# Forming the low halves of the expert weights on GpSimd instead of VectorE, and its high halves one step earlier

## The chip, the core and the metric

The kernel runs on one core of a Trainium2 chip. A core has five engines that run their own instruction streams and wait for each other on semaphores: TensorE (PE in the profile, with its weight loads as PEld), VectorE (DVE), ScalarE (ACT), GpSimd (POOL) and SyncE (SP, which only starts transfers here). The metric is device time in microseconds of one execution, the median of several. Smaller is better. TensorE writes to PSUM, the other memory is SBUF; in the profile a PSUM tensor of this kernel is called `bank`, everything else that a compute engine touches lies in SBUF.

## What is computed

A small language-model tower on 2 sequences of 2048 tokens: an embedding, a state-space mixer (Mamba-2 type) with a gated MLP, and a mixture of 8 experts with a shared one, at width 192. The change touches only how the weights of the last part are prepared.

```python
def _L0_ffn_ref(x, gate_weight, gate_bias, w1, w2, w3, sw1, sw2, sw3):
    ...
    h1 = jnp.einsum('td,eid->tei', x2, w1)
    h3 = jnp.einsum('td,eid->tei', x2, w3)
    h = jax.nn.silu(h1) * h3
    y = jnp.einsum('tei,edi,te->td', h, w2, cw)
    z = jax.nn.silu(x2 @ sw1.T) * (x2 @ sw3.T) @ sw2.T
    return (y + z).reshape(B, S, D)
```

Products with `w1`, `w3`, `sw1`, `sw3` and the router's weights are made on TensorE in float16. To keep float32 accuracy every weight matrix is held as two float16 parts: a high part (`w_hi`, the rounded weight) and a low part (`w_lo`, weight minus high part). A width of 192 is more than 128 partitions, so there is a second tensor for the rest of it: `wt_raw`, `wt_hi`, `wt_lo`. The columns COL_E to COLS, 2312 of them, belong to the shared expert, the eight experts and the router.

## The kernel before

**Staging.** The 2048 tokens are cut into 16 chunks of 128 (for both sequences at once). Each engine's program is `ramp()`, then `body(2, 1, 0)`, then a hardware loop over `body(i + 2, i + 1, i)` for i = 1 to 13, then `finale(14, 15)`. In `body(p, f, b)` three chunks are in work: chunk `b` is finished (MLP and experts), chunk `f` is in its scan, chunk `p` is begun (embedding, norm, input projection). The order of the instructions on each engine is written out by hand; nothing reorders them. A wait stops everything behind it on its engine.

**Preparing weights.** It happens once. The input projection's parts are made first in the ramp. The MLP's (`middle_weights`, 1536 columns) get their high part on ScalarE and their low part on VectorE (L1049), late in the ramp. The experts' high parts are made on GpSimd by `last_weights(hi, raw)` (L587 to L590): a copy of 2312 columns with conversion to float16, once for `w_hi` and once for `wt_hi`, as the last two instructions of GpSimd's ramp, behind `gate(0, 1)` and `halo(1)`. The experts' low parts are made on VectorE by its own `last_weights(wt, half)` (L1051 to L1057), four subtractions of 1156 columns each, which VectorE's `swiglu` (L1229 to L1250) places behind the gated products 0, 2, 3 and 5 of chunk 0 only (`not later(c)` is true in the first body alone). TensorE's `router` waits for all of them (`w_last_hi` 2, `w_last_lo` 4) before the first expert product of chunk 0.

**The work around it.** On VectorE: `convolve_tap` (xa, L1132) are the convolution taps of the new chunk, `masks` (mr, L1193) multiply the decay matrices `er` with the causal mask `gm` for the scan (units 0 to 5, 6 and 7 within `swiglu`, 8 to 11 behind it), `swiglu` forms `gt` from ScalarE's `sg` and a bank, `v_low` forms the low part of the MLP's input (v_t, L1071), `pre_low` that of the next chunk's input (u_t, the same line). On GpSimd: `decayed` (state, L503) and `gate` (y, L510) serve the scan, `weighted_x` (xw, L492) its state, `mixed` (rm, L516), `pre` and `norm2` (L445 and L447) are the powers of the three norms, `embed` (L458, L464) looks up the embedding rows by an indirect transfer. ScalarE's `mixed_norm` waits for rm; VectorE's `v_low` waits for it in turn; TensorE's `turn_v` and then `swiglu` wait for that. TensorE's first instruction of the scan of chunk 1 is the transposes of `scan_operands(1)` (L1647), which wait for ScalarE's `convolved_rest(1)` (xs, L716), which waits for the last tap (`xa_ready`).

Of the kernel before, what the change touches and what calls it, by code (L numbers as in the profile page):

```python
# [21 lines left out]
ALU = mybir.AluOpType  # L22
# [31 lines left out]
COL_E = COL_U + DM  # L54
# [25 lines left out]
def later(c):  # L80

    return not (isinstance(c, int) and c == 0)
# [20 lines left out]
def program(nc, tokens, position, table, weights, norms, conv_w, conv_b, shared_rows, d_skip, w_out, w_down,  # L103
            w2, identity, lower_ones, triangle_rows, exponent_rows, pair_rows, spread_rows, out):
    with ExitStack() as ctx:
# [332 lines left out]
        def _(pool):  # L438
# [67 lines left out]
            def gate(c, b):  # L506
                pool.wait_ge(y_sum[b], c + 1)
                pool.wait_ge(zs_ready[0], c + 1)
                pool.wait_ge(zs_ready[1], c + 1)
                pool.tensor_tensor(y[:, b], y[:, b], zs[:, :, b, :], ALU.mult).then_inc(y_ready[b], 1)  # L510
# [76 lines left out]
            def last_weights(hi, raw):  # L587
                x = slice(COL_E, COLS)
                pool.wait_ge(in_experts, 32)
                pool.tensor_copy(hi[:, x], raw[:, x]).then_inc(w_last_hi, 1)  # L590

            def ramp():
                pool.memset(xr[:, :, :, 0:KC - 1], 0.0).then_inc(setup_p, 1)
                embed(0)
                embed(1, 1)
                pre(0)
                keep(0)
                pool.memset(state[:], 0.0).then_inc(setup_p, 1)
                pool.memset(ones16[:], 1.0).then_inc(setup_p, 1)
                pool.memset(xd[:], 0.0).then_inc(setup_p, 1)  # L600
                pool.memset(bc[0:NS], 0.0).then_inc(setup_p, 1)
                pool.memset(bt[:, :, 0:NS], 0.0).then_inc(setup_p, 1)
                pool.wait_ge(setup_p, SETUP_P)
                pre(1)
                steps_decay(0)
                halo(0)
                embed(2)
                weighted_x(0, 0)
                weighted_x(0, 1)
                decayed(0, 0)  # L610
                steps_decay(1)
                gate(0, 0)
                decayed(0, 1)
                gate(0, 1)
                halo(1)
                last_weights(w_hi, w_raw)
                last_weights(wt_hi, wt_raw)

            def body(p, f, b):
                if f is not None:  # L620
                    weighted_x(f, 0)
                    weighted_x(f, 1)
                mixed(b)
                if f is not None:
                    pool.wait_ge(vl_turned, b + 1)
                    decayed(f, 0)
                    keep(f)
                    gate(f, 0)
                if p is not None:
                    pre(p)  # L630
                    embed(p + 1)
                norm2(b)
                if f is not None:
                    pool.wait_ge(xnt_done, b + 1)
                    decayed(f, 1)
                    gate(f, 1)
                if p is not None:
                    steps_decay(p)
                experts(b, p)
# [376 lines left out]
        def _(ve):  # L1016
# [31 lines left out]
                m = slice(COL_G, COL_E)  # L1048
                ve.scalar_tensor_tensor(lo[:, m], raw[:, m], scale, hi[:, m], ALU.mult, ALU.subtract).then_inc(w_rest_lo, 1)  # L1049

            def last_weights(wt, half):  # L1051

                ve.wait_ge(w_last_hi, 1 + wt)
                hi, lo, raw = (wt_hi, wt_lo, wt_raw) if wt else (w_hi, w_lo, w_raw)
                n = (COLS - COL_E) // 2
                x = slice(COL_E + half * n, COL_E + (half + 1) * n)
                ve.tensor_tensor(lo[:, x], raw[:, x], hi[:, x], ALU.subtract).then_inc(w_last_lo, 1)  # L1057

            def split(c, head, tail, src, hi, lo, lo_ready, lo_tail):


# [168 lines left out]
            def swiglu(c, p, f):  # L1230
                for t in range(NF):
# [13 lines left out]
                    if p is not None:  # L1245
                        if t == 1:
                            pre_add(p)
                            pre_stats(p)
                    if not later(c) and t in (0, 2, 3, 5):
                        last_weights(*divmod((0, 2, 3, 5).index(t), 2))  # L1250

            def second_input(c, src=p_out[0]):
                back_steps.start()
# [944 lines left out]
```

## Time and profile before

| | |
|---|---|
| three runs, median (lowest, highest) | 796.38 us (795.68 to 796.73) |
| the profiled execution, its own time | 796.69 us |
| its span in the profile | 794.9 us |
| busy in the span: PE, DVE, ACT, POOL | 757.6, 636.5, 546.8, 328.3 us |
| PE's share of the chain of work that ended last | 87% |

The span is what the engines' records cover; 1.8 us of the profiled execution's time lie outside it. Times in rows are microseconds from the span's start. In a timeline row the first number is the start, the second the duration (of the whole group if several instructions are merged, `x2`), and a bracket tells how long the engine had stood idle before and who released it. Ramp and first body take roughly the first 111 us; each further body takes some 46.6 us.

### The profile page before, as it was taken

The numbers are of one execution on the slowest core, as the hardware profiler recorded it, in microseconds if no ns is written. First come the engines' busy times: TensorE is split into PE (matmuls) and PEld (weight loads), VectorE is DVE, ScalarE is ACT, GpSimd is POOL, SyncE is SP. The second block draws the span as 40 slices with busy tenths as digits, with TensorE's granted clock in tenths as the row PEclk, the third lists the DMA queues.
The fourth block names the chain that finished last, engine by engine and source line by source line (L and its number), as shares of the span: only waits on it lengthen the run. The fifth ranks groups of instructions, "written<-read, shape, count | busy, mean of one in ns | idle before, by whom it ended". The sixth has DMA issues, their size and how long they took to land.

```text
span 794.9 us, 23059 instructions
## 1 busy us (share of the span) xinstructions
PE 757.6 (95%) x7278; PEld 646.6 (81%) x7278; DVE 636.5 (80%) x1691; ACT 546.8 (69%) x1242; POOL 328.3 (41%) x478
## 2 busy tenths in 40 slices
PE   2679999999999999999999999999999999999897
PEld 1556788988888898888888888888988888888786
DVE  4699987879788787978878797887889788786745
ACT  4975777767777776777767677776767777675533
POOL 5355544433444443344344334434443443442222
PEclk9899999999999999999999999999999999999999
DMA  7420000000000000000000000000000000000000
GB/s 251 155 89 1 12 22 12 9 25 6 15 10 21 10 6 25 3 17 10 21 10 6 25 3 17 10 21 10 6 24 4 17 10 16 14 6 11 2 1 21
DMA packets 14923, 18.93 MB, mean 24 GB/s; under 512 B 4656, under 2 KB 13008, under 8 KB 14448
## 3 DMA queue, kind: packets, MB, share of 16 engines
q1 hardware_dynamic: 13264, 15.25, 6.0%
q0 software_dynamic: 1632, 3.34, 1.7%
q8 instruction: 15, 0.25, 0.1%
q14 instruction: 12, 0.10, 0.0%
HBM read 14.39 MB, written 4.19 MB: 23 GB/s over the span
## 4 chain that ended last, share of the span: by engine, by line
PE 87%; DVE 2%; issue 1%; ACT 1%; POOL 0%; DVEq 0%; POOLq 0%; ACTq 0%
PE bank L1554 40%; PE bank L1934 11%; PE bank L1862 8%; PE bank L1718 6%; PE bank L1707 5%; PE bank L1831 4%; PE bank L1818 3%; PE bank L1809 3%; PE bank L1795 2%; PE bank L1647 1%; PE bank L1652 1%; PE bank L1691 1%; DVE mr L1193 1%; PE bank L1901 0%; PE bank L1902 0%
## 5 line engine op out<-in xcount | busy, mean ns | idle before, releaser
L1193 DVE SCALAR_TENSOR_TENSOR mr<-er,gm 128x512 f32<-128x512 f32 x192 | 125.8, 692 | 4.1 <-ACT er L782 3.7
L782 ACT ACTIVATE er<-bank 128x512 f32<-128x512 f32 x192 | 106.0, 595 | 27.4 <-PE bank L1707 27.1
L1934 PE MATMUL bank<-w2t,w_raw 128*128 128x192 f32 x576 | 112.6, 327 | 0.4 <-DVE w_raw L1362 0.4
L872 ACT ACTIVATE sg<-bank 128x256 f32<-128x256 f32 x144 | 55.1, 382 | 61.8 <-PE bank L1554 50.9
L1132 DVE SCALAR_TENSOR_TENSOR xa<-xr,cw_,xa 128x256 f32<-128x256 f32 x192 | 92.4, 488 | 6.3 <-ACT xa L690 4.7
L1934 PEld LDWEIGHTS bank<-w2t,w_raw 128*128 128x128 f32 x576 | 91.0, 190 | 1.8 <-DVE w_raw L1455 0.7
L1554 PE MATMUL bank<-x_h,wt_lo 128*128 128x256 f16 x288 | 78.5, 273 | 0.0
L1554 PE MATMUL bank<-x_h,w_lo 128*128 128x256 f16 x288 | 78.5, 273 | 0.0
L1554 PE MATMUL bank<-x_l,w_hi 128*128 128x256 f16 x288 | 78.5, 272 | 0.0
L1554 PE MATMUL bank<-x_h,w_hi 128*128 128x256 f16 x288 | 78.4, 272 | 0.0
L1554 PE MATMUL bank<-x_h,wt_hi 128*128 128x256 f16 x288 | 78.4, 272 | 0.0
L1862 PE MATMUL bank<-wd,gt 128*128 128x192 f32 x384 | 74.3, 329 | 1.4 <-DVE gt L1239 1.4
L566 POOL TENSOR_TENSOR w_raw<-w_raw 128x384 f32<-128x384 f32 x64 | 64.0, 1000 | 14.9 <-ACT w_raw L860 8.7
L821 ACT ACTIVATE sg<-bank 128x256 f32<-128x256 f32 x90 | 33.9, 376 | 51.5 <-PE bank L1554 51.5
L1362 DVE TENSOR_TENSOR w_raw<-sg,bank 128x256 f32<-128x256 f32 x144 | 59.9, 416 | 11.7 <-ACT sg L872 10.8
L1707 PE MATMUL bank<-ri,lj 128*128 128x512 f16 x192 | 63.7, 384 | 3.3 <-DMA ri<-sums 1.8
L1862 PEld LDWEIGHTS bank<-wd,gt 128*128 128x128 f32 x384 | 60.9, 190 | 2.6 <-DVE gt L1239 2.0
L1718 PE MATMUL bank<-mr,xd 128*32 128x128 f32 x1536 | 57.0, 283 | 1.6 <-DVE mr L1193 1.6
L503 POOL TENSOR_TENSOR state<-state,ends 128x384 f32<-128x384 f32 x31 | 31.8, 1027 | 64.1 <-PE bank L1569 38.3
L1455 DVE SCALAR_TENSOR_TENSOR w_raw<-bank,cw,w_raw 128x192 f32<-128x192 f32 x128 | 47.5, 413 | 10.4 <-POOL w_raw L566 7.5
L445 POOL TENSOR_SCALAR var<-mv 128x2 f32<-128x2 f32 x32 | 7.2, 225 | 113.1 <-DVE mv L1270 62.7
L1239 DVE TENSOR_TENSOR gt<-sg,bank 128x256 f32<-128x256 f32 x90 | 36.2, 414 | 21.9 <-ACT sg L821 21.9
(239 smaller groups left out, 2197.3 us busy)
## 6 DMA issues: line engine op xcount, KB each, us to landing
out<-w_raw SPq DMA_DIRECT2D x16, 192.0 KB, 2.0
pos<-position SPq DMA_DIRECT2D x16, 96.0 KB, 1.9
ri<-exponent_rows SPq DMA_DIRECT2D x1, 1536.0 KB, 6.4
w_raw<-weights SPq DMA_DIRECT2D x1, 1156.0 KB, 6.0
wt_raw<-weights SPq DMA_DIRECT2D x1, 1156.0 KB, 8.4
sums<-lj SPq DMA_DIRECT2D x16, 64.0 KB, 1.9
w2t<-w SPq DMA_DIRECT2D x1, 864.0 KB, 11.6
w_raw<-weights SPq DMA_DIRECT2D x1, 768.0 KB, 8.1
```

The costliest lines, as they stand in the source:

```text
L566: pool.tensor_tensor(acc[:], acc[:], wt_out[:, e % NWT], ALU.add).then_inc(acc_done, 1)
L782: act.activation(er[:, r % NER], p_d[r % 2][:].rearrange("p (h i) -> p h i", h=HG), ACT.Exp)\
L872: act.activation(sg[:, e % 4, :], src[e][:, 0:NB * Q], ACT.Silu).then_inc(sx_ready, 1)
L1132: ve.scalar_tensor_tensor(xa[:, m], xr[:, m, :, k:k + Q], cw_[:, m, k:k + 1], xa[:, m], ALU.mult, ALU.add)\
L1193: ve.scalar_tensor_tensor(mr[:, r % NMR], er[:, r % NER], 1.0, gm[:, r // NQ, :].unsqueeze(1).to_broadcast([128, HG, Q]), ALU.min, ALU.mult)\
L1362: ve.tensor_tensor(hh[:, e % NHH, :], sg[:, e % 4, :], src[e][:, NB * Q:2 * NB * Q], ALU.mult)\
L1455: ins = ve.scalar_tensor_tensor(acc[:, b], p_ex[e][:, b * D:(b + 1) * D], cw[:, b, e - 1:e], acc[:, b], ALU.mult, ALU.add)
L1554: ins = pe.matmul(out_, a, b, start=(i == 0), stop=(i == len(parts) - 1))
L1707: pe.matmul(p_d[r % 2][:].rearrange("p (h i) -> p h i", h=HG), lj[:, b, f, :], ri[:, of, b, f, :], start=True, stop=True).then_inc(d_done, 1)
L1718: ins = pe.matmul(p_y[row:row + 32, k * Q:(k + 1) * Q], xd[:, b, h, :], mr[:, r % NMR, heads.index(h), :], start=False, stop=(h % 2 == 1), ...
L1862: ins = pe.matmul(dst[:, b * D:(b + 1) * D], gt[:, f, b * Q:(b + 1) * Q], wd[:, f, :], start=(f == 0 and b == 0), stop=(f == NF - 1), skip ...
L1934: ins = pe.matmul(p_ex[e][:, b * D:(b + 1) * D], hh[:, e % NHH, b * Q:(b + 1) * Q], w2t[:, e, :], start=True, stop=True)
```

## The change

GpSimd gets a function `last_low(wt, half)` with the same subtraction of 1156 columns; VectorE's `last_weights` and its four calls are gone. GpSimd's two conversions stand elsewhere: the one for `w_hi` ahead of `gate(0, 1)`, the one for `wt_hi` between it and `halo(1)`. The four subtractions stand at the end of GpSimd's ramp, behind `mixed(0)`, behind `gate(1, 0)` and behind `pre(2)`, all in the ramp and the first body. TensorE's wait is the same. Nothing is computed otherwise.

```diff
+            def last_low(wt, half):
+                pool.wait_ge(w_last_hi, 1 + wt)
+                hi, lo, raw = (wt_hi, wt_lo, wt_raw) if wt else (w_hi, w_lo, w_raw)
+                n = (COLS - COL_E) // 2
+                x = slice(COL_E + half * n, COL_E + (half + 1) * n)
+                settle(pool)
+                pool.tensor_tensor(lo[:, x], raw[:, x], hi[:, x], ALU.subtract).then_inc(w_last_lo, 1)
+
             def ramp():
...
                 decayed(0, 1)
+                last_weights(w_hi, w_raw)
                 gate(0, 1)
+                last_weights(wt_hi, wt_raw)
                 halo(1)
-                last_weights(w_hi, w_raw)
-                last_weights(wt_hi, wt_raw)
+                last_low(0, 0)
 
             def body(p, f, b):
                 if f is not None:
                     weighted_x(f, 0)
                     weighted_x(f, 1)
                 mixed(b)
+                if not later(b):
+                    last_low(0, 1)
                 if f is not None:
                     pool.wait_ge(vl_turned, b + 1)
                     decayed(f, 0)
                     keep(f)
                     gate(f, 0)
+                if not later(b):
+                    last_low(1, 0)
                 if p is not None:
                     pre(p)
+                if not later(b):
+                    last_low(1, 1)
+                if p is not None:
                     embed(p + 1)
...
-            def last_weights(wt, half):
-
-                ve.wait_ge(w_last_hi, 1 + wt)
-                hi, lo, raw = (wt_hi, wt_lo, wt_raw) if wt else (w_hi, w_lo, w_raw)
-                n = (COLS - COL_E) // 2
-                x = slice(COL_E + half * n, COL_E + (half + 1) * n)
-                ve.tensor_tensor(lo[:, x], raw[:, x], hi[:, x], ALU.subtract).then_inc(w_last_lo, 1)
-
...
-                    if not later(c) and t in (0, 2, 3, 5):
-                        last_weights(*divmod((0, 2, 3, 5).index(t), 2))
```

GpSimd from the scan of chunk 0 (state is `decayed`, y is `gate`) over the end of its ramp to the first body's y, before:

```order
L503 TENSOR_TENSOR state<-state,ends 128x384 [waits yi_done1,eend_ready]
L510 TENSOR_TENSOR y<-y,zs 128x384 [waits zs_ready1,zs_ready0,y_sum1]
L483 COPY xr<-xr 128x8x3 [waits xa_ready]
L590 CAST w_hi<-w_raw 128x2312 [waits in_experts]
L590 CAST wt_hi<-wt_raw 128x2312 [waits in_experts]
L492 TENSOR_TENSOR xw<-xd,ends 128x384 [waits sn_done0,xd_ready0,eend_ready]
L492 TENSOR_TENSOR xw<-xd,ends 128x384 [waits sn_done1,xd_ready1,eend_ready]
L516 TENSOR_TENSOR rm<-vv,mhalf 128x2 [waits vv_ready]
L503 TENSOR_TENSOR state<-state,ends 128x384 [waits yi_done0,s_ready0,eend_ready,vl_turned]
```

The same stretch of GpSimd now:

```order
L503 TENSOR_TENSOR state<-state,ends 128x384 [waits yi_done1,eend_ready]
L590 CAST w_hi<-w_raw 128x2312 [waits in_experts]
L510 TENSOR_TENSOR y<-y,zs 128x384 [waits zs_ready1,zs_ready0,y_sum1]
L590 CAST wt_hi<-wt_raw 128x2312 [waits in_experts]
L483 COPY xr<-xr 128x8x3 [waits xa_ready]
L598 TENSOR_TENSOR w_lo<-w_raw,w_hi 128x1156 [waits w_last_hi]
L492 TENSOR_TENSOR xw<-xd,ends 128x384 [waits sn_done0,xd_ready0,eend_ready]
L492 TENSOR_TENSOR xw<-xd,ends 128x384 [waits sn_done1,xd_ready1,eend_ready]
L516 TENSOR_TENSOR rm<-vv,mhalf 128x2 [waits vv_ready]
L598 TENSOR_TENSOR w_lo<-w_raw,w_hi 128x1156 [waits w_last_hi]
L503 TENSOR_TENSOR state<-state,ends 128x384 [waits yi_done0,s_ready0,eend_ready,vl_turned]
```

Both conversions moved up past the copy of the halo, one of them past the y product as well, and two subtractions stand behind the halo and behind rm.

GpSimd further on in the first body, from its y product (`gate(1, 0)`) over the norm of chunk 2 (var0 and r0) to the embedding of chunk 3, before:

```order
L510 TENSOR_TENSOR y<-y,zs 128x384 [waits zs_ready1,zs_ready0,y_sum0]
L445 TENSOR_SCALAR var0<-mv 128x2 [waits stat_ready]
L447 TENSOR_TENSOR r0<-var0,mhalf 128x2 [waits pre_p]
L458 TENSOR_SCALAR row<-tok 128x2 [waits tokens_in,emb_in]
L464 DMA emb<-table,row 128x192 [waits row_ready,h0_ready]
```

The same stretch now:

```order
L510 TENSOR_TENSOR y<-y,zs 128x384 [waits zs_ready1,zs_ready0,y_sum0]
L598 TENSOR_TENSOR wt_lo<-wt_raw,wt_hi 128x1156 [waits w_last_hi]
L445 TENSOR_SCALAR var0<-mv 128x2 [waits stat_ready]
L447 TENSOR_TENSOR r0<-var0,mhalf 128x2 [waits pre_p]
L598 TENSOR_TENSOR wt_lo<-wt_raw,wt_hi 128x1156 [waits w_last_hi]
L458 TENSOR_SCALAR row<-tok 128x2 [waits tokens_in,emb_in]
```

One subtraction stands ahead of that norm, one behind it and ahead of the embedding.

VectorE in the first body's `swiglu` (gt are the gated products, mr the scan's masks, h_next the embedding of chunk 2), before:

```order
L1239 TENSOR_TENSOR gt<-sg,bank 128x256 [waits sg_ready]
L1193 SCALAR_TENSOR_TENSOR mr<-er,gm 128x512 [waits yq_done,e_ready]
L1057 TENSOR_TENSOR w_lo<-w_raw,w_hi 128x1156 [waits w_last_hi]
L1239 TENSOR_TENSOR gt<-sg,bank 128x256 [waits sg_ready]
L1089 SCALAR_TENSOR_TENSOR h_next<-emb,pos 128x384 [waits h0_copied,position_in,emb_in]
```

Of the four subtractions of VectorE this is the first; all four are gone, and nothing else moved on VectorE, TensorE or ScalarE.

## Rows read from the trace of the kernel before

**Rows 1.** Two windows, TensorE's swiglu to router, first and second body: length, PE busy, PEld, DVE, ...

```profile
70.27:91.11 20.84, 19.25 (x191) 15.96 (x192) 19.03 (x43) 13.07 (x25) 10.99 (x11) 1.00 0.04 11
119.18:137.66 18.48, 18.48 (x194) 16.00 (x195) 14.21 (x39) 12.98 (x25) 7.36 (x11) 1.00 0.05 13
```

**Rows 2.** Chain that ended last, first body: start, duration, engine and line.

```profile
73.72 1.35 DVE w_lo L1057
...
77.92 1.27 DVE w_lo L1057
...
80.78 1.27 DVE wt_lo L1057
...
82.44 1.58 PE bank L1862 x8
```

**Rows 3.** The same chain in the second body: projection of dt after the MLP.

```profile
130.56 0.24 PE bank L1554 x10
```

**Rows 4.** Timeline of GpSimd, end of the ramp and first body.

```profile
48.81 1.18 POOL L503 TENSOR_TENSOR state<-state,ends 128x384 f32<-128x384 f32 x1 [0.40 <-PE bank L1809]
53.75 1.16 POOL L510 TENSOR_TENSOR y<-y,zs 128x384 f32<-128x384 f32 x1 [3.76 <-DVE y L1213]
...
58.10 2.11 POOL L590 CAST wt_hi<-wt_raw 128x2312 f16<-128x2312 f32 x1
60.17 4.65 POOL L492 TENSOR_TENSOR xw<-xd,ends 128x384 f32<-128x384 f32 x2
64.79 1.17 POOL L516 TENSOR_TENSOR rm<-vv,mhalf 128x2 f32<-128x2 f32 x1
...
71.72 1.00 POOL L510 TENSOR_TENSOR y<-y,zs 128x384 f32<-128x384 f32 x1 [0.63 <-DVE y L1213]
```

**Rows 5.** Timeline of VectorE over the same time.

```profile
50.93 1.28 DVE L1193 SCALAR_TENSOR_TENSOR mr<-er,gm 128x512 f32<-128x512 f32 x2
...
53.59 2.13 DVE L1132 SCALAR_TENSOR_TENSOR xa<-xr,cw_,xa 128x256 f32<-128x256 f32 x3
...
58.47 3.35 DVE L1049 SCALAR_TENSOR_TENSOR w_lo<-w_raw,nrm,w_hi 128x1536 f16<-128x1536 f32 x1
...
62.07 2.05 DVE L1049 SCALAR_TENSOR_TENSOR wt_lo<-wt_raw,nrm,wt_hi 128x1536 f16<-128x1536 f32 x1
64.05 1.33 DVE L1193 SCALAR_TENSOR_TENSOR mr<-er,gm 128x512 f32<-128x512 f32 x1
...
68.17 0.74 DVE L1071 SCALAR_TENSOR_TENSOR v_t<-bank,rm,v_t 128x192 f16<-128x192 f32 x2
...
73.12 0.68 DVE L1193 SCALAR_TENSOR_TENSOR mr<-er,gm 128x512 f32<-128x512 f32 x1
```

**Rows 6.** Timeline of ScalarE and TensorE, end of the ramp and first body.

```profile
55.75 0.63 ACT L716 ACTIVATE xs<-xa 128x512 f32<-128x512 f32 x1 [2.11 <-DVE xa L1132]
56.70 1.25 PE L1647 MATMUL bank<-idf,xs 128*128 128x128 f32 x6 [3.84 <-issue]
64.21 0.20 ACT L802 ACTIVATE vv<-ss 128x2 f32<-128x2 f32 x1
65.47 0.60 ACT L782 ACTIVATE er<-bank 128x512 f32<-128x512 f32 x1 [0.57 <-PE bank L1707]
```

**Rows 7.** Window 58 to 60: the number behind POOL's busy time is TensorE's granted clock.

```profile
58.00:60.00 2.00, 2.00 (x10) 1.41 (x9) 2.00 (x2) 1.73 (x5) 2.00 (x2) 0.50 0.00 0
```

**Rows 8.** Timeline of the second body: r0 on GpSimd, u_t on VectorE.

```profile
125.22 0.69 POOL L447 TENSOR_TENSOR r<-var,mhalf 128x2 f32<-128x2 f32 x1
127.09 0.76 DVE L1071 SCALAR_TENSOR_TENSOR u_t<-uc,r,u_t 128x192 f16<-128x192 f32 x2 [1.12 <-ACT u_t L841]
```

**Rows 9.** Single lines over the whole run: shortest, median, longest in ns.

```profile
L534 POOL TENSOR_TENSOR ap_<-dt_,aexp x16: 287/307/347, 21.8 to 698.1; 128x48 f32<-128x48 f32 x16
L566 POOL TENSOR_TENSOR w_raw<-w_raw x64: 993/1000/1005, 105.9 to 787.9; 128x384 f32<-128x384 f32 x64
L1340 DVE SCALAR_TENSOR_TENSOR e_w<-e_rank,g_sc x16: 175/878/883, 99.1 to 779.9; 128x16 f32<-128x16 f32 x16
```

## The prediction, written before the changed kernel ran

> **What bounds the kernel now.** Read the windows first, then the chain, then the timelines of VectorE and GpSimd side by side. From the second body on TensorE is busy all the time: 18.48 us of the 18.48 between the start of `swiglu` and the router [rows 1]. No change on another engine can shorten that. The first body needs 20.84 us for the same TensorE work, and TensorE is busy in 19.25 of it [rows 1]. The chain says why: three of VectorE's four subtractions of 1156 columns stand on it, at 73.72, 77.92 and 80.78, with TensorE taking over at 82.44 [rows 2]. They cost 1.27 us each there, 3.8 together, but as the second body shows only 20.84 - 18.48 = 2.36 us can be won by removing them; after that TensorE is next.
>
> **What GpSimd and VectorE do to each other.** The price of the change is in the rows of 58 to 65 us. GpSimd's conversion runs from 58.10 and the next instruction starts at 60.17; VectorE's subtraction of 1536 columns was issued at 58.47 and needed 3.35 us, to 61.82 [rows 4, 5]. If it stood still until 60.17 it ran 1.65 us. Then GpSimd's two xw need 4.65 us, where a product of this size has 1.00 [rows 4, 9]: the first fits if it stood until 61.82, ran to 62.5, and VectorE's second subtraction (issued 62.07, 2.05 us) stood until then; the second xw stood until 64.1, ran to 64.8, and the mask at 64.05 (1.33 us instead of 0.64, half of the pair at 50.93) stood until then [rows 5]. All lengths come out within 0.1 us. The three taps at 53.59 beside the y product at 53.75 and the small e_w (0.175 alone, 0.878 as its median, 16 times) fit too [rows 4, 5, 9]. So an instruction of GpSimd and one of VectorE that has two SBUF inputs exclude each other for their whole length, and the one issued first goes first. Instructions of VectorE with a bank as one input are not hit. The Trainium skill says the same (SBUF — State Buffer, section Who interferes with whom: an exclusive lock, held for the whole instruction); this is the rule that speaks against the change, the trace agrees with it in the 3.35 and 4.65 us above, and nothing in the sum needs it. What follows is this bookkeeping carried through the new order.
>
> **Price of a subtraction on GpSimd, D.** No row has it. Two-input products take 0.307 us for 48 columns and 1.000 for 384 [rows 9]: 2.06 ns per column, so 1.000 + 772 x 0.00206 = 2.6 us for 1156. I take 2.55. Simple proportion to the 384 columns gives 3.0; the shortest fitting rate, that of the freed xw (0.7 us for 384 columns, as read above [rows 4]), 2.1. The Trainium skill (GPSIMD Engine Reference, section 3.1) has 4497 ns for 2048 columns; an estimate in proportion is 2.54 us, and the sum by it would be the same; no row here shows it.
>
> **Step by step**, in the trace's own times.
> - *Conversion of w_hi.* It can start when `decayed(0, 1)` ends, 48.81 + 1.18 = 49.99, behind a mask that VectorE has in work until about 50.5; 2.05 us, to 52.55. The mask pair of 50.93 stands until then: +1.6 us for it, for the last products of the scan, for y on VectorE, and so for GpSimd's y product (53.75, now 55.35) [rows 4, 5]. TensorE has nothing else to do there: it was idle for 3.84 us before 56.70 [rows 6].
> - *Conversion of wt_hi.* It now comes right behind the y product, before the last of three taps. The taps were done at 53.59 + 2.13 = 55.72 [rows 5]; now the second one ends at 56.8, the conversion runs to 58.85 and the third tap ends at 59.3: **+3.55 us**. ScalarE's xs (55.75, released by that tap) and TensorE's transposes (56.70) wait for it and shift by as much [rows 6].
> - *Subtraction 1* runs from the halo copy, 59.6 to 62.15, while VectorE works on banks. It is hidden. VectorE's 1536 columns, issued at 62.0, now find no conversion in front: 62.15 to 63.8, xw to 64.5, the second 1536 columns to 66.1, xw to 66.85, first mask to 67.45. Before it was 64.05 + 1.33 = 65.38, so of 3.55 us **+2.07** are left.
> - *Subtraction 2.* TensorE and ScalarE are still 3.55 late: vv is ready at 64.41 + 3.55 = 67.96, rm (1.17 us) at 69.27 [rows 4, 6]. Masks 1 to 3 end at 69.25; the fifth needs er, 66.07 + 3.55 = 69.62 [rows 6]. So GpSimd asks 0.4 us ahead of it and holds until 69.27 + 2.55 = 71.82. Fifth mask to 72.45, v_low at 72.85 instead of 68.17 [rows 5]: **+4.65** for the turned input, for ScalarE and for TensorE's `swiglu`, which starts at 74.9 instead of 70.27.
> - *Subtraction 3.* GpSimd's y product (71.72 + 1.00) ends at 77.37; the mask behind the first gated product (73.12) would be issued at 77.77 [rows 4, 5]. It stands until 79.9, +2.15 us against a body without the subtractions, and all of VectorE's queue with it: gated products, embedding, statistics, and behind them GpSimd's `pre`.
> - *Subtraction 4.* In the second body r0 is done at 125.91 and VectorE's u_t starts at 127.09, 6.73 and 7.91 us after `swiglu` [rows 1, 8]. With 74.9 and 2.15 added, GpSimd holds from 83.8 to 86.35 and u_t, due at 84.95, waits: +1.4, and 0.1 more for the row computation that slips in between its halves. Together 3.65 us, of which I let TensorE swallow 0.4 (it never waits in the second body; 0 to 0.5). There the dt projection starts 130.56 - 119.18 = 11.38 us after `swiglu` [rows 1, 3]; now 11.38 + 3.25 = 14.63, where it was 82.44 + 1.58 - 70.27 = 13.75 [rows 1, 2]: **+0.9**.
> - *Removed:* VectorE's four subtractions; their gain is inside the last figure, which starts from the second body. *Nothing late behind it:* the low parts are ready at 86.4, some 10 us ahead of the router. The embedding's transfers end near 90.4 and GpSimd is free before the second norm's statistics at about 91.3; this cover is 0.9 us, and a later r2 would delay TensorE about one to one.
>
> **Sum.** 4.65 + 0.9 = +5.5 us. Everything later is bound by TensorE and shifts whole. Against the profiled execution (span 794.9, time 796.69) that is 802.2; the median of the runs is 0.3 lower, so **801.9 us**. D counts three times: 2.1 gives 4.1, 3.0 gives 6.9 (the first subtraction then counts a little too). Own range 800.4 to 803.6.
>
> **Rivals.**
> - *The idle time is real* (faster). Had GpSimd's work no hold on VectorE, or only where VectorE does not ask, the first body would take 18.48 instead of 20.84 us: 794.0. For it: GpSimd is busy 10.99 of those 20.84 us. Against: the 3.35, 4.65 and 1.33 us rows; it would need the masks not to be hit, yet the one at 64.05 was. It decides on whether a mask beside a subtraction lasts 0.7 or some 2.8 us. Chance 0.09.
> - *Lucky order* (slower, by less). Two races are close: 0.4 us at 69.3 and 0.4 us at 77.4. If VectorE's mask is first in one or both, the hold falls on a later instruction, behind work on banks: 0.7 to 2 us less each, 798.5 to 800.4. Chance 0.11.
> - *TensorE's clock* (slower still). It was granted 0.50, the 1.2 GHz level, in 58 to 60 us, behind 3.84 us of idleness [rows 6, 7]. That gap grows by about 2 us. I take the slow stretch as merely shifted; if it lasts longer the exponents, not the masks, set the pace, at up to 1 to 2 us; or r2 comes late. 803.6 to 805. Chance 0.08.
> - *No effect*, the subtractions and conversions balancing out within 0.2%: no single mechanism; 0.02.
> - The forecast: 0.70.
>
> **Numbers.** The range is 798.4 to 804.6; it leaves out the faster case, no change and the far end of the clock's. A measurement of this kernel tells about 0.2%, 1.6 us, from no change. Faster 0.09, same 0.04, slower 0.87.
>
> **What would show it.** Step by step: TensorE's transposes near 60.2 instead of 56.70 with the last tap as releaser; a tap of some 2.4 us; GpSimd's subtraction at 2.5 us; one mask each of about 2.7 us before v_low and behind the first gated product; a u_t pair of 2 us; `swiglu` at 74.9 and the dt projection at 89.5. Masks of 0.7 us beside a subtraction of GpSimd would prove me wrong, as would taps still done by 56.

## The result: slower by 0.5%

Changed kernel: 798.98 us median of 6 runs (798.55 to 801.06). Kernel before, beside it: 795.44 us (794.49 to 796.73). Ratio 1.0049, 95% interval [1.0033, 1.0065]; the medians lie 3.5 us apart. The time lies in the predicted range of 798.4 to 804.6, 2.9 us under the predicted value. It lies outside the narrower range of the forecast itself, 800.4 to 803.6, and in that of the rival "lucky order". The profiled execution took 801.06 us with a span of 799.2; before it was 796.69 and 794.9.

### The profile after

In the changed kernel's text the lines of VectorE, ScalarE and TensorE stand 6 to 16 lower: the mask L1193 is now L1201, the tap L1132 is L1140, VectorE's subtraction of 1536 columns L1049 is L1065, u_t L1071 is L1079, er L782 is L798. GpSimd's subtraction is L598.

The windows first, of the ramp's end and of TensorE's first `swiglu` up to the router; columns as in [rows 1] (length, PE, PEld, DVE, ACT, POOL, TensorE's granted clock, DMA):

```profile
56.00:58.00 2.00, 0.00 (x0) 0.00 (x0) 1.97 (x2) 0.00 (x0) 2.00 (x2) 0.50 0.12 35
...
62.00:64.00 2.00, 1.54 (x8) 0.86 (x6) 2.00 (x4) 1.46 (x6) 0.78 (x1) 0.50 0.00 0
64.00:66.00 2.00, 1.89 (x8) 1.60 (x9) 2.00 (x3) 1.32 (x3) 2.00 (x2) 0.70 0.00 0
...
74.83:95.69 20.86, 19.16 (x194) 15.93 (x191) 17.00 (x39) 12.87 (x25) 12.06 (x13) 1.00 0.04 11
```

That stretch lasts 20.86 us as against 20.84 [rows 1]. VectorE is busy 2 us less in it, and it bought nothing: what the four subtractions had cost there came back as waiting. All of the loss was there already when `swiglu` started, 74.83 instead of 70.27.

The timeline of GpSimd, answering to [rows 4]:

```profile
49.96 2.57 POOL L590 CAST w_hi<-w_raw 128x2312 f16<-128x2312 f32 x1
55.22 1.16 POOL L510 TENSOR_TENSOR y<-y,zs 128x384 f32<-128x384 f32 x1 [2.69 <-DVE y L1221]
56.33 2.30 POOL L590 CAST wt_hi<-wt_raw 128x2312 f16<-128x2312 f32 x1
...
59.25 2.37 POOL L598 TENSOR_TENSOR w_lo<-w_raw,w_hi 128x1156 f16<-128x1156 f32 x1
...
68.57 0.72 POOL L516 TENSOR_TENSOR rm<-vv,mhalf 128x2 f32<-128x2 f32 x1 [1.83 <-ACT vv L818]
69.28 2.57 POOL L598 TENSOR_TENSOR w_lo<-w_raw,w_hi 128x1156 f16<-128x1156 f32 x1
...
77.28 2.37 POOL L598 TENSOR_TENSOR wt_lo<-wt_raw,wt_hi 128x1156 f16<-128x1156 f32 x1
...
83.27 2.38 POOL L598 TENSOR_TENSOR wt_lo<-wt_raw,wt_hi 128x1156 f16<-128x1156 f32 x1
```

And VectorE's, answering to [rows 5]:

```profile
50.95 2.73 DVE L1201 SCALAR_TENSOR_TENSOR mr<-er,gm 128x512 f32<-128x512 f32 x2
...
55.06 3.85 DVE L1140 SCALAR_TENSOR_TENSOR xa<-xr,cw_,xa 128x256 f32<-128x256 f32 x3
...
68.91 3.48 DVE L1201 SCALAR_TENSOR_TENSOR mr<-er,gm 128x512 f32<-128x512 f32 x2 [0.42 <-ACT er L798]
...
72.79 0.74 DVE L1079 SCALAR_TENSOR_TENSOR v_t<-bank,rm,v_t 128x192 f16<-128x192 f32 x2
...
77.73 2.47 DVE L1201 SCALAR_TENSOR_TENSOR mr<-er,gm 128x512 f32<-128x512 f32 x1
```

Read the two side by side. Across from each conversion or subtraction of GpSimd but one stands a row of VectorE that grew: the mask pair at 50.95 (2.73 us, was 1.28), the three taps at 55.06 (3.85, were 2.13), the masks at 68.91 (two in 3.48, undisturbed 1.3), the mask at 77.73 (2.47, was 0.68), and the u_t pair at 84.41 (1.80; 0.76 in the second body before). Only the subtraction at 59.25 meets nobody: VectorE then works on banks and waits for TensorE. The chain of waits shows u_t as the last of them, and then TensorE's dt projection at 88.76, which was at 84.02:

```profile
84.41 0.10 DVE u_t L1079
84.51 1.28 issue
85.79 0.43 DVE u_t L1079
...
88.76 0.24 PE bank L1560 x10
```

The 1.28 us of "issue" in the middle of u_t is the wait for the subtraction of 83.27, which ends at 83.27 + 2.38 = 85.65. TensorE's transposes, answering to [rows 6]:

```profile
59.90 1.51 PE L1653 MATMUL bank<-idf,xs 128*128 128x128 f32 x6 [5.75 <-issue]
```

### The profile page after: what moved, and what is told of

The parts are those of the page before. It is cut to its first block, busy times and chain, and to the rows that moved or that the text cites. A ratio compares the mean times of both kernels' runs of the same rounds, so it can differ in the third digit from the quotient of the medians.

```text
span 799.2 us, 23063 instructions
## 1 busy us (share of the span) xinstructions
PE 757.7 (95%) x7278; PEld 646.9 (81%) x7278; DVE 638.0 (80%) x1687; ACT 546.0 (68%) x1242; POOL 332.8 (42%) x482
## 3 DMA queue, kind: packets, MB, share of 16 engines
q1 hardware_dynamic: 13264, 15.25, 5.9%
## 4 chain that ended last, share of the span: by engine, by line
PE 89%; issue 3%; DVE 3%; ACT 3%; POOL 1%; DMA 1%; DVEq 0%; POOLq 0%; ACTq 0%; SPq 0%
PE bank L1560 40%; PE bank L1940 11%; PE bank L1868 8%; PE bank L1724 6%; PE bank L1713 5%; PE bank L1837 4%; PE bank L1824 3%; PE bank L1815 3%; PE bank L1801 2%; PE bank L1653 1%; PE bank L1658 1%; PE bank L1697 1%; DVE mr L1201 1%; DVE xa L1140 1%; ACT er L798 1%
## 5 line engine op out<-in xcount | busy, mean ns | idle before, releaser
L1201 DVE SCALAR_TENSOR_TENSOR mr<-er,gm 128x512 f32<-128x512 f32 x192 | 131.4, 719 | 4.4 <-ACT er L798 4.0
L798 ACT ACTIVATE er<-bank 128x512 f32<-128x512 f32 x192 | 105.9, 596 | 26.3 <-PE bank L1713 26.1
L1140 DVE SCALAR_TENSOR_TENSOR xa<-xr,cw_,xa 128x256 f32<-128x256 f32 x192 | 94.0, 496 | 6.4 <-ACT xa L706 4.8
L566 POOL TENSOR_TENSOR w_raw<-w_raw 128x384 f32<-128x384 f32 x64 | 63.9, 998 | 14.9 <-ACT w_raw L876 8.7
```

What stands on the lines that cost most here:

```text
L566: pool.tensor_tensor(acc[:], acc[:], wt_out[:, e % NWT], ALU.add).then_inc(acc_done, 1)
L798: act.activation(er[:, r % NER], p_d[r % 2][:].rearrange("p (h i) -> p h i", h=HG), ACT.Exp)\
L1140: ve.scalar_tensor_tensor(xa[:, m], xr[:, m, :, k:k + Q], cw_[:, m, k:k + 1], xa[:, m], ALU.mult, ALU.add)\
L1201: ve.scalar_tensor_tensor(mr[:, r % NMR], er[:, r % NER], 1.0, gm[:, r // NQ, :].unsqueeze(1).to_broadcast([128, HG, Q]), ALU.min, ALU.mult)\
```

## The experiments

**1. The conversions alone.** The kernel before, with only the two conversions in their new places.

```diff
                 decayed(0, 1)
+                last_weights(w_hi, w_raw)
                 gate(0, 1)
+                last_weights(wt_hi, wt_raw)
                 halo(1)
-                last_weights(w_hi, w_raw)
-                last_weights(wt_hi, wt_raw)
```

> The kernel before with GpSimd's two conversions in their new places (ahead of the second y product, and between it and the halo copy); the four subtractions stay on VectorE. Holds theory (one engine's instruction keeps the other's two-input SBUF instruction out for its whole length): the last tap ends near 58.9 instead of 55.72, the transposes start near 59.9 instead of 56.70; of those 3.2 us about 2.3 are left at TensorE's swiglu (rm at 69.3, fifth mask done at 70.1 instead of 67.78), and the first body is as long as before. +2.3 us, ratio 1.003. Rival, that only the subtractions cost something in the changed kernel and the conversions sit in idle time: +0 us, ratio 1.000, taps done by 56.

798.13 us (8 runs), 1.0027 [1.0016, 1.0037]. VectorE's timeline:

```profile
49.94 2.73 DVE L1193 SCALAR_TENSOR_TENSOR mr<-er,gm 128x512 f32<-128x512 f32 x2
...
54.05 3.85 DVE L1132 SCALAR_TENSOR_TENSOR xa<-xr,cw_,xa 128x256 f32<-128x256 f32 x3
...
68.22 1.29 DVE L1193 SCALAR_TENSOR_TENSOR mr<-er,gm 128x512 f32<-128x512 f32 x2 [0.73 <-ACT er L782]
```

The same 2.73 and 3.85 as in the changed kernel, so these two holds belong to the conversions, and the masks at 68.22 are free when no subtraction stands beside them. This execution's ramp ran about 1 us earlier than the others', so its transposes (58.89) are to be read with that 1 us added; experiment 8 comes back to this.

**2. The subtractions alone.** The changed kernel, with the conversions back behind the halo copy.

```diff
                 decayed(0, 1)
-                last_weights(w_hi, w_raw)
                 gate(0, 1)
-                last_weights(wt_hi, wt_raw)
                 halo(1)
+                last_weights(w_hi, w_raw)
+                last_weights(wt_hi, wt_raw)
                 last_low(0, 0)
```

> The changed kernel with the two conversions back in their old places behind the halo copy; only the subtractions are on GpSimd. Holds theory, carried through: the first subtraction is issued at 60.17 and is held until VectorE's first 1536 columns end at 61.82, holds until 64.2; the second 1536 columns end near 65.8, first mask near 67, rm near 69.2, the second subtraction runs about 69.8 to 72.1, fifth mask to 73.3, v_low at 73.9 to 74.4 instead of 68.17: swiglu +5.5 us, and the first body as in the changed kernel: +5 to +6 us, ratio 1.007, more than the whole change. Rival, that the parts add up (whole change +4.3 in its profile, conversions +2.3): +2 us, ratio 1.0025.

800.74 us (5 runs), 1.0064 [1.005, 1.0077]. The transposes stand at 56.66, as before, and yet `swiglu` starts only at 76.08. GpSimd:

```profile
60.13 3.88 POOL L598 TENSOR_TENSOR w_lo<-w_raw,w_hi 128x1156 f16<-128x1156 f32 x1
63.97 3.59 POOL L492 TENSOR_TENSOR xw<-xd,ends 128x384 f32<-128x384 f32 x2
67.53 1.17 POOL L516 TENSOR_TENSOR rm<-vv,mhalf 128x2 f32<-128x2 f32 x1
68.68 2.87 POOL L598 TENSOR_TENSOR w_lo<-w_raw,w_hi 128x1156 f16<-128x1156 f32 x1
```

and VectorE over the same time:

```profile
62.03 3.60 DVE L1065 SCALAR_TENSOR_TENSOR wt_lo<-wt_raw,nrm,wt_hi 128x1536 f16<-128x1536 f32 x1
65.54 6.55 DVE L1201 SCALAR_TENSOR_TENSOR mr<-er,gm 128x512 f32<-128x512 f32 x5
```

Here the first subtraction is not hidden: it queues behind the conversions, and both engines wait for each other in turn from 58 to 71 us, five masks taking 6.55 us where five undisturbed ones take 3.1. The parts therefore don't add: by the ratios the conversions alone cost 2.1 us, the subtractions alone 5.1, both together 3.9 and 4.4 (the two measurements of the changed kernel). Beside the subtractions, the new place of the conversions costs 3 us at the taps and saves more than that behind them.

**3. Each subtraction in four pieces** of 289 columns, all else as in the changed kernel.

```diff
-                n = (COLS - COL_E) // 2
-                x = slice(COL_E + half * n, COL_E + (half + 1) * n)
-                settle(pool)
-                pool.tensor_tensor(lo[:, x], raw[:, x], hi[:, x], ALU.subtract).then_inc(w_last_lo, 1)
+                n = (COLS - COL_E) // 8
+                for i in range(4):
+                    at = COL_E + (half * 4 + i) * n
+                    x = slice(at, at + n)
+                    settle(pool)
+                    ins = pool.tensor_tensor(lo[:, x], raw[:, x], hi[:, x], ALU.subtract)
+                    ins.then_inc(w_last_lo, 1)
...
-                    pe.wait_ge(w_last_lo, 4)
+                    pe.wait_ge(w_last_lo, 16)
```

> The changed kernel with each of GpSimd's subtractions cut into four of 289 columns. The work on GpSimd grows (about 0.8 us a piece, 3.3 for four), the longest hold shrinks to 0.8 us. Holds theory: no mask or u_t stands longer than about 0.9 us beyond its length; swiglu starts near 73.2 instead of 74.9, the whole comes to about +2.5 us, ratio 1.003. Rival, that the amount of GpSimd work beside VectorE's counts and not the length of one instruction: as the changed kernel or slower, ratio 1.005 or more.

798.38 us (7 runs), 1.0032 [1.0021, 1.0043]. VectorE waits for one piece instead of a whole subtraction, and GpSimd's four pieces stretch instead (2.8 us alone, 3.7 and 3.8 where VectorE comes between them):

```profile
66.41 3.73 DVE L1204 SCALAR_TENSOR_TENSOR mr<-er,gm 128x512 f32<-128x512 f32 x5
...
75.58 1.38 DVE L1204 SCALAR_TENSOR_TENSOR mr<-er,gm 128x512 f32<-128x512 f32 x1
...
77.21 0.75 DVE L1100 SCALAR_TENSOR_TENSOR h_next<-emb,pos 128x384 f32<-128x384 f32 x1
...
82.21 1.33 DVE L1082 SCALAR_TENSOR_TENSOR u_t<-uc,r,u_t 128x192 f16<-128x192 f32 x2 [1.39 <-ACT u_t L860]
83.44 1.22 DVE L1204 SCALAR_TENSOR_TENSOR mr<-er,gm 128x512 f32<-128x512 f32 x1
```

The pieces cost these instructions 0.2 to 0.6 us each (h_next 0.75 instead of 0.55, the u_t pair 1.33 instead of 0.76, the mask at 83.44 1.22 instead of 0.68). The mask at 75.58 stood behind GpSimd's y product (75.41, 1.00 us), not behind a piece. `swiglu` starts at 72.58, 12.24 us after the transposes, as against 14.93 in the first profile of the changed kernel. The gain in the whole is less sure: the interval of this ratio overlaps with those of the changed kernel, 1.0049 and 1.0055.

Some of it was lost again on GpSimd's own queue: its decayed state came behind the last piece, and VectorE's new state waited for it.

```profile
74.18 0.56 DVE L1230 TENSOR_TENSOR state<-state,bank 64x384 f32<-64x384 f32 x1 [1.41 <-POOL state L503]
```

**4. GpSimd as long busy, but reading nothing.** Each subtraction is replaced by a memset of all 2312 columns of the same low part, so each low part is zeroed twice; the low parts are left out of the computation.

```diff
-                n = (COLS - COL_E) // 2
-                x = slice(COL_E + half * n, COL_E + (half + 1) * n)
+                x = slice(COL_E, COLS)
+                if half:
+                    pool.wait_ge(w_last_lo, 2 * wt + 1)
                 settle(pool)
-                pool.tensor_tensor(lo[:, x], raw[:, x], hi[:, x], ALU.subtract).then_inc(w_last_lo, 1)
+                pool.memset(lo[:, x], 0.0).then_inc(w_last_lo, 1)
```

> The changed kernel with each subtraction on GpSimd replaced by setting the 2312 columns of that low part to zero: it writes SBUF and reads nothing. The low parts of the expert weights are left out of the products, which changes the numbers and no instruction of TensorE. If GpSimd's reads make the hold, masks beside it take 0.7 us, swiglu starts near 72.6 (the conversions' share stays), the first body takes 18.5 us from swiglu to router as the second one does: 0 us against before, ratio 1.000 (0.999 to 1.001). Rival, that any instruction of GpSimd on SBUF makes the hold: masks stand for the length of the writes, and the whole is slower by 2 to 4 us.

796.07 us (10 runs), 1.0003 [0.9992, 1.0013]. GpSimd and VectorE at the places of the second and third subtraction:

```profile
68.22 2.01 POOL L599 MEMSET w_lo<- 128x2312 f16 x1
...
74.02 2.02 POOL L599 MEMSET wt_lo<- 128x2312 f16 x1
```

```profile
67.86 1.29 DVE L1202 SCALAR_TENSOR_TENSOR mr<-er,gm 128x512 f32<-128x512 f32 x2 [0.53 <-ACT er L799]
...
74.49 0.68 DVE L1202 SCALAR_TENSOR_TENSOR mr<-er,gm 128x512 f32<-128x512 f32 x1
```

GpSimd is busy at the same places for 2.0 us instead of 2.4, and the masks beside it last 0.65 and 0.68 us. So it is not GpSimd's being busy that stops VectorE, nor a semaphore: it is that the subtraction reads SBUF. One input is enough, as the conversions of experiment 1 show, which read one tensor and hold too. The Trainium skill (SBUF — State Buffer, section Who interferes with whom) says so too: VectorE with two SBUF inputs contends with a GpSimd instruction that reads SBUF, not with one that only writes it. From `swiglu` to dt this kernel needs 11.4 us (71.62 to 83.04), the second body's pace, against 13.9: all that the change hoped for is there once the hold is gone. The conversions still hold the ramp back and eat most of these 2.5 us: by experiment 1 they cost 2.1. (`swiglu` starts at 71.62 instead of 70.27, in an execution whose transposes, at 58.74, were about 1 us early.) The 0.4 us that are left are too little for the runs to show.

**5. The low parts on VectorE, at its idle places.** The kernel before, with the four calls moved: one ahead of the first gated product, one ahead of u_t, two behind the last gated product.

```diff
             def swiglu(c, p, f):
+                if not later(c):
+                    last_weights(0, 0)
                 for t in range(NF):
...
+                    if not later(c) and t == 3:
+                        last_weights(0, 1)
...
-                    if not later(c) and t in (0, 2, 3, 5):
-                        last_weights(*divmod((0, 2, 3, 5).index(t), 2))
+                    if not later(c) and t == 5:
+                        last_weights(1, 0)
+                        last_weights(1, 1)
```

> The kernel before with VectorE's four subtractions kept on VectorE but put where the second body shows it idle: one ahead of the first gated product (1.1 us idle), one ahead of u_t (1.1 us idle), two behind the last gated product (1.3 us idle). Bound by TensorE as the second body (18.48 us instead of 20.84) but for the second one at the end, which delays the norm by some 0.9 us: -1.2 us, ratio 0.9985. Rival, that idle time of VectorE in the first body is not there once the others move: within 0.1%.

795.48 us (11 runs), 0.9996 [0.9987, 1.0005]: no difference that the runs show, as the rival had it. Counted between TensorE's first matmuls, it won 2.1 us from `swiglu` to dt (11.5 instead of 13.6), and lost 1.3 from dt to the router (8.5 instead of 7.2). The chain names what is late there, the two subtractions ahead of the second norm:

```profile
79.90 2.54 DVE wt_lo L1057 x2
82.44 0.48 DVE h L1262
```

**6. The conversions on ScalarE**, in three pieces, and all subtractions at idle places of VectorE; GpSimd does nothing for these weights.

```diff
-                last_weights(w_hi, w_raw)
-                last_weights(wt_hi, wt_raw)
...
+            def last_high(hi, raw, x):
+                act.wait_ge(in_experts, 32)
+                act.copy(hi[:, x], raw[:, x]).then_inc(w_last_hi, 1)
...
```

> Nothing of this weight work on GpSimd: the conversions on ScalarE (half of wt_hi and all of w_hi around the silu of chunk 1's first channels, where ScalarE is idle 1.4 and 2.1 us, half of wt_hi ahead of v_h), the subtractions on VectorE in four idle places (ahead of xd of chunk 1, ahead of the first gated product, ahead of u_t, behind the last gated product). VectorE's 1536 columns then last 1.7 us each, no conversion in front, worth up to 0.9 us at swiglu; the first body takes 18.6 us: -2.9 us, ratio 0.9965. Rival, that ScalarE's conversions delay the scan by as much: -1 us or no gain.

794.92 us (11 runs, beside 795.45 for the kernel before), 0.9998 [0.9989, 1.0007]. Missed: I expected 0.9965. The profile does show dt at 80.13 instead of 84.02, and some 1.3 us of these 3.9 are the earlier ramp of that execution. By the last body 1.2 us of it were gone again, about 0.07 per body. At the start of every body TensorE's weight load waits for VectorE's weighed sum 0.52 us instead of 0.41, and VectorE for GpSimd's sum. Why the medians show nothing of what is left, I could not settle.

**7. The halo copy later in each body.** That waiting chain suggested moving GpSimd's halo copy from behind the first expert sum to behind the fourth, in the kernel before and in experiment 6.

```diff
-                    if e == 0 and p is not None:
+                    if e == NP - 2 and p is not None:
                         halo(p)
```

> The kernel before, but in every body GpSimd copies the halo behind the fourth sum of the experts instead of behind the first. In the trace of before GpSimd stands 5.8 us in each body in front of that copy while three products it could add are ready, VectorE's weighed sums wait 0.5 us for its last sum, and TensorE's first product of the next body 0.4 us for them, 14 times. If that wait is real, each body is 0.4 us shorter: -5 us, ratio 0.994. Rival: the sums, two-input instructions of 1 us, now hold VectorE's taps and TensorE waits for these instead: 1.000 or slower.

> The kernel with conversions on ScalarE and subtractions in VectorE's idle places, with the halo copy behind the fourth sum as well. Its profile had reached the second body 3.9 us ahead of the kernel before and lost 1.3 us of that over the following bodies, waiting 0.5 us for VectorE's sums at the start of each. If that is where the gain goes, both gains add: -7.5 us, ratio 0.9905. Rival: the lead is lost in another way, and this kernel is no more than 1 us ahead of the one with the later halo copy alone.

811.15 us (5 runs), 1.0203 [1.0188, 1.0218], and 808.31 us (5 runs), 1.017 [1.0154, 1.0186]. Both missed by far, with the rival of the first one right: the halo copy had been what held GpSimd's sums back until VectorE's taps were through. Now they run beside the taps, which were pairs of 1.00 and 0.87 us:

```profile
197.64 1.62 DVE L1132 SCALAR_TENSOR_TENSOR xa<-xr,cw_,xa 128x256 f32<-128x256 f32 x2
...
199.51 2.04 DVE L1132 SCALAR_TENSOR_TENSOR xa<-xr,cw_,xa 128x256 f32<-128x256 f32 x2
```

Each body got 1.1 us longer. It is the same hold as in the change, met at another place. The rival of the second kernel did not come true: that kernel is 2.8 us ahead of the first in the medians, and 3.5 us ahead in the profiles from the second body to the last. So the gain of experiment 6, which the medians hide beside the kernel before, is there beside the kernel with the later halo copy; why in one pair and not in the other stays open.

**8. The two kernels once more,** unchanged, each under a new name, to see how far single executions differ.

> The kernel before, unchanged, profiled and timed again as a control. If the ramp varies from one execution to the next, its transposes start near 55.5 as in the two kernels with the work off GpSimd, instead of 56.70, and the rest is the same from there; if not, 56.70 again and the two kernels' 1.1 us is theirs. Ratio 1.000 either way.

> The changed kernel, unchanged, profiled and timed again beside the others. Holds theory: ratio 1.0045 to 1.006 and the same long masks; the runs seen so far lie in two groups 2 us apart, so its profile may come out 2 us shorter than the 799.2 of the first, with the difference in the ramp (clock or transfers) and not in the four holds.

795.84 us (10 runs, 1.0003 [0.9994, 1.0012]) and 799.26 us (6 runs, 1.0055 [1.0038, 1.0073]). The second profile of the kernel before has its transposes at 56.61, nearly where the first has them (56.70). Yet experiment 5, the same program up to `swiglu`, had them at 55.59, and experiments 1, 4 and 9 had theirs about 1 us ahead of the two profiles of the changed kernel: a ramp can be 1 us shorter in one execution than in another. The second profile of the changed kernel differs from the first mainly at one place. VectorE there:

```profile
65.73 3.73 DVE L1201 SCALAR_TENSOR_TENSOR mr<-er,gm 128x512 f32<-128x512 f32 x5
...
70.50 1.75 DVE L1201 SCALAR_TENSOR_TENSOR mr<-er,gm 128x512 f32<-128x512 f32 x1
```

The fifth mask was issued ahead of the second subtraction (68.83 here), and so the hold fell on the sixth, with work on banks between. The transposes are at 59.67, nearly as in the first profile, but `swiglu` is at 72.74 instead of 74.83 and dt at 86.29 instead of 88.76. What differs ahead of that place is TensorE's clock, which was back 2 us earlier, 0.87 where the first profile has 0.50:

```profile
62.00:64.00 2.00, 1.33 (x9) 0.83 (x8) 2.00 (x3) 1.48 (x5) 1.01 (x1) 0.87 0.00 0
```

The first er was started at 64.08 instead of 64.73, the fifth was done at 68.4 instead of 69.4, and rm was done at 68.85 instead of 69.28, for it stood behind a mask (1.24 us instead of 0.72). So the fifth er came 1 us earlier, and the subtraction's turn only 0.45 us.

**9. That race decided by hand,** once for each side: GpSimd's second subtraction waits until the fifth mask is done, or the fifth mask waits until the subtraction is done.

```diff
                 if not later(b):
+                    pool.wait_ge(m_ready, NR + 5)
                     last_low(0, 1)
```

> The changed kernel with one wait more: GpSimd's second subtraction waits until VectorE's fifth scan mask of chunk 1 is done, so that VectorE always wins the race of about 0.4 us at 69 us. Race theory: the upper of the two groups of the changed kernel's runs (800.0 to 801.5) is the one in which the subtraction came first, and it disappears: all runs between 797.8 and 799.4, median 798.6, ratio to before 1.0035 to 1.0045; in the profile the first five masks are undisturbed, the subtraction holds the sixth one (1.8 instead of 0.67 us), and swiglu starts 2.1 us ahead of where it did in the profiled run of the changed kernel, relative to the transposes (13.1 after them instead of 14.9). Rival (the two groups have another cause, TensorE's clock at the end of the ramp or noise that the kernel before has too): both groups stay, median near 799.1 and ratio 1.005.

```diff
-                    masks(f, range(5))
+                    if later(b):
+                        masks(f, range(5))
+                    else:
+                        masks(f, range(4))
+                        ve.wait_ge(w_last_lo, 2)
+                        masks(f, (4,))
```

> The changed kernel with the race forced the other way: VectorE's fifth scan mask of chunk 1 waits until GpSimd's second subtraction is done. Race theory: only the upper group is left, 799.8 to 801.5, median 800.7, ratio to before 1.006 to 1.007; swiglu starts 14.9 us behind the transposes, and the distance to the kernel with the mask first is 2.1 us. Rival (another cause): both groups stay, or the two forced kernels differ by less than 1 us.

Mask first: 798.80 us (6 runs, 798.15 to 801.27), 1.0041 [1.0025, 1.0057]. Subtraction first: 801.88 us (6 runs, 800.47 to 802.68), 1.0073 [1.006, 1.0086]. The hold moved as expected; VectorE with the mask first, and with the subtraction first:

```profile
68.14 1.29 DVE L1202 SCALAR_TENSOR_TENSOR mr<-er,gm 128x512 f32<-128x512 f32 x2 [0.79 <-ACT er L799]
...
70.47 2.10 DVE L1202 SCALAR_TENSOR_TENSOR mr<-er,gm 128x512 f32<-128x512 f32 x1
```

```profile
71.04 0.69 DVE L1201 SCALAR_TENSOR_TENSOR mr<-er,gm 128x512 f32<-128x512 f32 x1 [2.28 <-POOL w_lo L598]
```

The order is worth 3.1 us in the medians and 1.35 in these two executions (transposes to dt 27.84 and 29.19 us); I had expected 2.1. From the transposes to `swiglu` I had expected 13.1 and 14.9 us, and it was 14.29 and 15.25: TensorE's clock came back late in both. With the mask first:

```profile
62.00:64.00 2.00, 1.44 (x5) 0.76 (x4) 2.00 (x3) 1.29 (x4) 1.91 (x2) 0.50 0.00 0
64.00:66.00 2.00, 2.00 (x11) 1.91 (x11) 2.00 (x2) 1.00 (x3) 1.60 (x1) 0.80 0.00 0
```

So the mask-first order has been seen with both clocks, and this tells what the clock costs by itself: the fifth mask ended 10.67 us after the transposes here, and 9.79 in the second profile of the changed kernel, 0.9 us apart. In both forced kernels rm was done just before the fifth er (68.52 and 68.60; 68.45 and 68.52), so in experiment 11's profile it was the added wait that put the mask first.

Eight of the changed kernel's 12 runs lie below 799.3, where no run with the subtraction first does. Against the kernel before beside it, the changed kernel's medians are 3.5 us later both times, the mask first 2.4 and the subtraction first 5.5: they lie between the two orders, nearer to the mask first, as a mixture would. Which order each run had is not shown; only two of the 12 have a profile, one of each order. Missed in part: with the mask first two runs were still at 799.9 and 801.3, so the race is not all of the spread. The kernel before spreads nearly as far, 794.2 to 797.1 in the runs beside experiment 8, and what does that stays open.

## The prediction, step by step

**The hold**: right in every row that was to show it. In us: the mask pair predicted +1.6, measured 2.73 - 1.28 = +1.45; the taps' end +3.55, measured 58.91 - 55.72 = +3.19; the transposes +3.55, measured +3.20; the first subtraction hidden, and it was; the fifth mask's end 72.45, measured 72.39; `swiglu` 74.9, measured 74.83. That the last two agree within 0.1 us is partly luck: the transposes came 0.35 us earlier than predicted and rm took 0.72 us instead of 1.17, and the slow clock, which I had not counted, took 0.8 us back (8.29 us from the transposes to vv instead of 7.51). Experiments 1 and 2 put these holds down to the conversions and subtractions one by one, experiment 4 takes them away with GpSimd as busy as before. The rival "the idle time is real" (794.0) fell at the point named for it: a mask beside a subtraction lasts 2.5 to 2.8 us. 

**D, the subtraction's length**: mis-sized by little. 2.37 us alone (at 59.25, 77.28 and 83.27), I took 2.55. I said that D counts three times; but the second subtraction stood behind a mask and lasted 2.57, so the shorter D shows only in the last two, 0.36 us, and these are part of the next term.

**From `swiglu` to dt**: the term was too large, 14.63 us, measured 88.76 - 74.83 = 13.93. The mask behind the first gated product cost 2.47 - 0.68 = 1.8 instead of 2.15, since D was shorter. The u_t pair cost 1.80 - 0.76 = 1.04 instead of 1.5; its subtraction ended at 85.65 instead of 86.35. Both losses together are 2.8 us, of which TensorE swallowed 0.3; I had 0.4. So the sum at dt is +4.7 instead of +5.5, and the profiled execution +4.4 (801.06 - 796.69) instead of +5.5.

**Which order a run has**: the forecast is 2.9 us above the median, in two parts. The profiled execution had the order that I forecast and took 801.06 instead of 802.2; these 1.1 us are the sizes above. The other 1.8 us are the step from that execution to the median, for which I took 0.3 off where 2.1 were measured. Some of that has nothing to do with the order: the kernel before's profiled execution, too, lies 1.25 us above its median (795.44 from six runs; I had 796.38 from three). The rest, 0.8 us, fits the race at 69.3 us, which I saw, and to whose other outcome I gave 0.11, with 798.5 to 800.4 for it; both measured medians lie in there. I had worked out both engines' times from one profile, and the lead of 0.4 us is no more than what two executions differ by. A lead of that size deserved a chance near one half, not one in nine.

That my 801.9 is the time of the kernel in which the subtraction is forced to be first, 801.88, is luck: in the profiled execution with that very order the steps came to +4.4 us, not +5.5. The second race, at 77.4, was won by the mask in the second profile (75.27 behind a mask at 74.80) and gained 0.4 us only (13.55 instead of 13.93 from `swiglu` to dt): the hold fell on h_next instead, 2.21 us where 0.55 is undisturbed.

**TensorE's clock**: I took the slow stretch as merely shifted, and that was wrong. The granted clock was 0.50 from 56 to 64 us and 0.70 to 66, where before it was 0.90 again from 60; TensorE had been idle for 5.75 us ahead of its transposes instead of 3.84. The rival had the mechanism right: with the same order, the later return costs 0.9 us (experiment 9), just under its 1 to 2, and it moves er and rm as well, between which the race is decided. Its total was wrong, since the other terms were too large. The late return is not the change's alone, though. The second profile of the kernel before has 0.50 until 62, 0.96 in the next 2 us, and vv 8.42 us after the transposes, but `swiglu` starts 13.52 us after them as against 13.57 in the first: there the masks, held by xw, are as late as that anyway.

**Hidden costs**: as named. The low parts were ready at 85.7, ten us ahead of the router, and neither the embedding nor the second norm behind it shows on the chain between dt and the router, which takes no longer than before: 7.09 us between TensorE's first matmuls of the two (88.60 to 95.69), as against 7.24 (83.86 to 91.10).

## What to carry to other kernels

Idle time of GpSimd is usable only where VectorE at that moment reads banks, waits, or has slack: read the two timelines side by side and give each GpSimd instruction with SBUF inputs the VectorE instruction that it will stop. An instruction moved to another engine costs its new length at the worst place, so a long one in short pieces holds less at each place (experiment 3, where the gain in the whole is within the intervals), but look at what is queued behind the pieces. Where two engines ask within half a microsecond of each other, forecast both orders and give them even chances; one profile doesn't tell which one the median has.

## What the runs showed of the hardware

GpSimd's subtraction of an f32 and an f16 input takes 2.37 us for 1156 columns and 0.70 for 289 (four in 2.81, experiment 3), which is 1.93 ns per column and about 0.14 us fixed. That is a little less than its f32 products, from whose 2.06 ns and 0.2 us I had worked out 2.6 us. The conversion of 2312 columns takes 2.05 to 2.1. A memset of 2312 f16 columns, 2.01 us, leaves VectorE's masks at 0.65 and 0.68 us, though it writes the tile that the subtraction wrote. And who stands waiting is served next: in experiment 2 the two engines took turns without a gap from 58 to 71 us, each instruction's row lasting about as long as the other engine's one plus its own.

The hold works the other way too. In the kernel before, the two instructions of GpSimd that start the indirect transfers of the embedding took 2.94 and 1.81 us at 80.10 and 83.34, beside VectorE's subtractions of 1156 columns; in the changed kernel, without these, they took 1.11 and 0.96.
